# Metaformer kernel on one core: block 0 normalised by POOL, first maxima moved ahead of block 1's products, router chains reordered

## The reference, cut to what matters

```python
x = x + _L0_conv_ref(_ln_c(x), ...)   # attention in windows of 14 x 14 (padded), 12 heads of 16, relative positions
t = t + _L0_ffn_ref(_ln_t(t), ...)    # 8 experts, best 2 of each token, 192 -> 768 -> 192, gelu
x = x + _L1_conv_ref(_ln_c(x), ...)   # attention over 3 x 3 neighbours at dilations 1, 2, 3
t = t + _L1_ffn_ref(_ln_t(t), ...)    # 8 experts, best 2, weights normalised
def _ln_c(v, eps=1e-06): return (v - mean(v)) / sqrt(var(v) + eps)      # over the 192 channels
attn = softmax(q * scale @ k + rel_h + rel_w)                            # of the first attention
gates = softmax(x_flat @ Wg + bg); topk_g, topk_i = top_k(gates, 2)      # the router
```

## Time and profile before

| what | us |
|---|---|
| median of three runs | 894.55 |
| profiled execution | 897.03 |
| its span | 895.2 |
| TensorE busy in the span | 787.2 (88%) |
| VectorE, ACT, POOL busy | 422.8, 311.8, 364.8 |
| first scores (L792) | 73.90 |
| logits of router 0 read (L1215) | 272.49 |
| logits of router 1 read (L1215) | 669.05 |

### The profile page before, as it was taken

The page is one execution under the profiler, slowest core; times in us unless marked ns, Lnnn a source line. Parts: engine busy times, 40 slices in busy tenths (PEclk is TensorE's granted clock), DMA queues, the critical chain, the costliest instruction groups (busy, mean ns, idle before and its releaser), DMA issues.

```text
span 895.2 us, 19348 instructions
## 1 busy us (share of the span) xinstructions
PE 787.2 (88%) x6140; PEld 666.0 (74%) x6141; DVE 422.8 (47%) x1000; ACT 311.8 (35%) x862; POOL 364.8 (41%) x795
## 2 busy tenths in 40 slices
PE   6997999999986999999992589998786999999990
PEld 3775888888773799999991359783673899999980
DVE  7243545557637433333324516997338333333325
ACT  3332545455524233333331550012240333333330
POOL 5862354340130666666652130000032566666640
PEclk8685899999986999999997599999997999999995
DMA  7492564565382111111114089500971111111116
GB/s 222 108 240 67 130 142 123 145 158 103 133 327 95 45 46 46 45 51 50 51 38 141 1 217 232 80 24 27 322 266 72 38 51 48 48 51 46 45 28 211
DMA packets 60858, 96.50 MB, mean 108 GB/s; under 512 B 26223, under 2 KB 44356, under 8 KB 60808
## 3 DMA queue, kind: packets, MB, share of 16 engines
q1 hardware_dynamic: 42248, 59.60, 24.3%
q0 software_dynamic: 18560, 36.24, 13.9%
HBM read 65.51 MB, written 31.52 MB: 108 GB/s over the span
## 4 chain that ended last, share of the span: by engine, by line
PE 64%; DVE 15%; issue 6%; DMA 5%; POOL 4%; ACT 3%; SPq 2%; DVEq 0%; POOLq 0%
PE ps L1398 14%; PE ps L1406 10%; PE ps L1410 7%; PE ps L1774 4%; PE ps L747 3%; PE ps L723 3%; DVE x_sb L1340 2%; PE ps L772 2%; PE ps L1389 2%; PE ps L1792 2%; PE ps L792 2%; DVE arena L1686 2%; PE ps L380 2%; PE ps L816 2%; PE ps L858 1%
## 5 line engine op out<-in xcount | busy, mean ns | idle before, releaser
L1440 ACT ACTIVATE arena<-ps,b1s 128x128 f32<-128x128 f32 x468 | 129.5, 376 | 254.4 <-PE ps L1410 153.8
L1398 PE MATMUL ps<-arena 128*128 x936 | 165.4, 327 | 1.5 <-DVE rt L1305 1.5
L1398 PEld LDWEIGHTS ps<-arena 128*128 128x128 f32 x936 | 150.3, 190 | 2.4 <-issue 2.1
L1406 PE MATMUL ps<-xnT 128*128 128x128 f32 x936 | 117.5, 275 | 3.0 <-DVE xnT L1298 3.0
L1406 PEld LDWEIGHTS ps<-xnT 128*128 128x128 f32 x936 | 114.4, 192 | 4.0 <-DVE xnT L1298 4.0
L272 POOL TENSOR_TENSOR rstd<-veps,cst 128x4 f32<-128x4 f32 (+1 forms) x10 | 11.5, 1154 | 201.5 <-DVE veps L266 201.5
L603 DVE TENSOR_REDUCE rt<-ps 98x2 f32<-98x392 f32 x96 | 53.2, 563 | 79.7 <-PE ps L772 79.5
L1454 POOL TENSOR_TENSOR credit<-credit 1x1 f32<-1x1 f32 x306 | 57.8, 189 | 77.0 <-DVE rt L1305 34.3
L1462 POOL DMA_INDIRECT xnT<-xnd,gcur x78 | 78.6, 1007 | 16.2 <-issue 14.9
L1007 ACT ACTIVATE arena<-ps 98x392 f32<-98x392 f32 x96 | 47.0, 499 | 84.6 <-PE ps L792 84.0
L1410 PE MATMUL ps<-xnT,rt 64*128 64x128 f32 x936 | 73.2, 289 | 0.0
(11 more groups left out here) (215 smaller groups left out, 1310.2 us busy)
## 6 DMA issues: line engine op xcount, KB each, us to landing
arena<-in_w SPq DMA_DIRECT2D x16, 576.0 KB, 7.6
arena<-in_w1a SPq DMA_DIRECT2D x16, 384.0 KB, 6.0
arena<-yd SPq DMA_DIRECT2D x8, 768.0 KB, 7.1
kk<-kd SPq DMA_DIRECT2D x48, 96.0 KB
qq<-qd SPq DMA_DIRECT2D x16, 264.0 KB
qd<-arena POOLq DMA_DIRECT2D x16, 224.0 KB, 5.8
qq<-qd SPq DMA_DIRECT2D x16, 192.0 KB
arena<-in_w1b SPq DMA_DIRECT2D x16, 192.0 KB, 6.5
```

Of the source, the lines that this page charges most:

```text
L1398: last = mm(ps[:, DOWN, 0:C], hidT[r][:, f, :], w2s[:, e, f, :], start=f == 0, stop=f == FT - 1)
L1406: mm(hidden(r, f), wcura[r][:, f * P:(f + 1) * P], xgT[:, 0, :], start=f < 2, stop=False, skip_group_check=True)
L1440: last = nc.scalar.activation(hidT[r][:, f, :], hidden(r, f), ACT.Gelu, bias=b1s[l][:, bass.ds(e * FT + f, 1)])
```

## The change

1. Block 0's inverse root is taken by POOL's power, as everywhere else; ACT's root and VectorE's reciprocal go. SP loads `cst` second, the key constants later. VectorE scales the query/key weights after the tiles. POOL waits with its casts until the tiles are done; the power of blocks 1 to 3 comes after block 0's t2. ACT's first key rows come after the first relative rows. Two of nine first fillers go.
2. SP issues block 0's stores of t0, t2, r0, r1.
3. TensorE starts on the maxima right after block 1's t0; t2 and the pieces of r0 and r1 follow between units (`between`), and the fillers go. The bank list follows. ACT copies r1 of block 1 after the first exponentials.
4. In router 0, only the moments stay in step 7; the tiles come after all slots. TensorE's tail has another order, and the transposes alternate between banks 2, 3 and 0, 1.
5. In router 1, ACT copies block 3's values before it normalises block 0; transposes run a block ahead of the logits, in banks 6, 7 and 0, 1, with fillers of half the columns; twelve fillers, not nine, stand before the first transposes.

The diff, cut to its core:

```diff
         def ln_refine(v, n, bs):
...
-            if n == 0:
-                nc.vector.reciprocal(r, r).then_inc(s_("ln_inverse"), 1)
-                v.wait_ge(s_("ln_inverse"), turn)
...
+        def nx_bank(l, b):
+            return (2, 0)[b % 2] if l == 0 else (6, 0)[b % 2]
...
-            if b:
-                pe.wait_ge(s_("nx_copied"), 2 * (l * BLKS + b))
+            if b >= 2:
+                pe.wait_ge(s_("nx_copied"), 2 * (l * BLKS + b - 1))
+            if l == 1 and b == 1:
+                pe.wait_ge(s_("proj1_out"), 3)
...
+            for kind in ("t0", "t2", "r0", "r1"):
+                sp.wait_ge(s_("split"), split_at(kind, 0))
+                store(sp, kind, 0)
             sp.wait_ge(s_("q_rows"), CPB + 1)
             for cc in range(CPB):
                 load(0, cc)
...
             nc.gpsimd.memset(q0[32:64].bitcast(F32), 0.0).then_inc(s_("q_rows"), 1)
+            pool.wait_ge(s_("cst_in"), 16)
+            pool.wait_ge(s_("q_rows"), 1)
+            ln_power(pool, 0, first)
             pool.wait_ge(s_("cq_in"), 16)
-            pool.wait_ge(s_("q_rows"), 1)
+            pool.wait_ge(s_("xn_ready"), 1)
...
                 heads_split("t2", b)
+                if b == 0:
+                    ln_power(pool, 0, rest)
...
                 if b == BLKS - 1 and s == 7:
                     v.wait_ge(s_("misc_full"), max(FULL["x1", b], FULL["r2", b]))
-                    ln_moe(v, 0, range(BLKS - 1))
+                    ln_moments(v, 1, range(BLKS - 1))
...
+            moe_normalise(v, 0, range(BLKS - 1))
             normalise(BLKS - 1, 2)
...
-            keep_clock(BANK["r2", 0], 9)
+            keep_clock(BANK["r2", 0], 7)
...
             queries_and_keys(1, 0)
-            queries_and_keys(1, 2)
-            relatives(1, 0)
-            relatives(1, 1)
...
+            def between(H, u):
+                if (H, u) == (0, 2):
+                    queries_and_keys(1, 2)
+                if H == 2 and u < 2:
+                    relative(1, 0, u)
+                if (H, u) == (HC, 0):
+                    transposed_maxima(0)
+                if H == HC and u:
+                    relative(1, 0, u + 1)
+                if H == HC + 1 and u < 2:
+                    relative(1, 1, u)
+                if H == HC + 2 and u < 2:
+                    relative(1, 1, u + 2)
+
             for H in range(AHEAD):
                 for u in range(UNITS):
                     scores_for_max(H, u)
-                    mm(ps[:, PV, 0:2 * P], trib, maskb[:, 0, 0:2 * P], start=True, stop=True)
-                if H == HC:
-                    transposed_maxima(0)
+                    between(H, u)
...
-            nx_transpose(pe, 0, 0)
             transposed_outputs(BLKS - 1, 0)
             for part in range(2):
                 values_product(GROUPS - 1, part)
+            nx_transpose(pe, 0, 0)
+            token_major(BLKS - 1, 2)
             nx_transpose(pe, 0, 1)
-            token_major(BLKS - 1, 2)
+            transposed_outputs(BLKS - 1, 1)
             router_logits(pe, 0, 0, 0, 2)
-            transposed_outputs(BLKS - 1, 1)
-            router_logits(pe, 0, 0, 2, TPB)
             projection(BLKS - 1, 0)
             projection(BLKS - 1, 1)
+            router_logits(pe, 0, 0, 2, TPB)
             router_logits(pe, 0, 1)
             nx_transpose(pe, 0, 2)
+            mm(ps[:, PV, :], ident, cst[:, 0:BT], start=True, stop=True)
             router_logits(pe, 0, 2)
...
-            act.wait_ge(s_("ck_in"), 16)
-            for cc in range(2):
-                key_rows(cc)
-            ln_sqrt(act, 0, first)
...
             round_heads(0, 0)
-            ln_sqrt(act, 0, rest)
             round_heads(0, 2)
             copy_relative(0, 0)
+            act.wait_ge(s_("ck_in"), 16)
+            for cc in range(2):
+                key_rows(cc)
...
+                nx_transpose(pe, l, 0)
                 for b in range(BLKS):
-                    nx_transpose(pe, l, b)
-                    mm(ps[:, 5, :], ident, cst[:, 0:BT], start=True, stop=True)
+                    if b + 1 < BLKS:
+                        nx_transpose(pe, l, b + 1)
+                    mm(ps[:, 5, 0:BT // 2], ident, cst[:, 0:BT // 2], start=True, stop=True)
...
-            for _ in range(9):
+            for _ in range(12):
                 nc.tensor.matmul(ps[:, 4, :], ident, cst[:, 0:BT], start=True, stop=True)
...
-            for b in range(3):
+            for b in range(BLKS):
                 copy_values(b)
             block_normalise(act, 3, 0)
-            copy_values(3)
```

More of the change, by code:

```diff
@@ L491, in split_at, with store @@
             return b * len(SPLIT) + SPLIT.index(kind) + 1
+        def store(eng, kind, b):
+            for to, rows, heads, src, m, p0, p1 in stores(kind):
+                eng.dma_start(to[b, rows, heads].rearrange("r h n -> h r n"), src[p0:p1, m].bitcast(F32))\
+                    .then_inc(s_(f"{STORED[kind]}{b}"), 16)
         def first_matrices(sp, l, lo, hi):
@@ L541, in attn0_pool @@
         def attn0_pool(pool):
-            def store(kind, b):
-                for to, rows, heads, src, m, p0, p1 in stores(kind):
-                    pool.dma_start(to[b, rows, heads].rearrange("r h n -> h r n"), src[p0:p1, m].bitcast(F32))\
-                        .then_inc(s_(f"{STORED[kind]}{b}"), 16)
             def heads_split(kind, b):
@@ L1071, in attn0_scalar @@
             copy_relative(1, 0)
-            copy_relative(1, 1)
             def slot_a(b, s):
```

50 lines of the change are left out of this document (25 added, 25 removed).

## The result

Four runs of the changed kernel took 876.38, 879.18, 880.49 and 889.12 us (median 879.84), four of the kernel before 893.41 to 896.85 (median 895.28): ratio 0.9846, 95% interval [0.9809, 0.9883]. Six more runs of it later took 874.67 to 891.44 (0.9872 [0.9831, 0.9913]); all ten have a median of 882.9. So the change makes the kernel faster, by 12 to 15 us (under 2%, but clear of noise); forecast were 24.3. Medians here are over all runs of a kernel; the ratios leave out those over 1.5% above its fastest (three of the six of "late maxima", and one each of the changed kernel again, of "fillers before the maxima loop" and of "POOL stores").

The account below looks back on a forecast made before the run. TensorE was taken to bound the kernel (64% of the chain of waits, DMA 5%). Gains 11.9 + 4 + 3.7 + 4.7 = 24.3 took the profiled 897.03 to 872.7, less 2.5 to the median: 870.3 us, range 861 to 881.

Parts of the forecast that it names:

- the term of 4: First heads, 70 to 97 us: without the 5.30 us wait the stretch may run at full clock; 4 us, bounds 0 and 8.
- the step from the profiled execution to the median: End of the sum: the profiled execution before lay 2.5 us over its median, so 872.7 becomes 870.3.
- Part 1: Block 0's normalisation: transposes start at 9.6 us, not 16.20; window-order products at 17.2, not 25.74, 8.5 earlier.
- The rule on shared ports: Front: VectorE's two-input SBUF sum and POOL's SBUF reads exclude each other; POOL's splits may stand 3.2 us, otherwise nothing.
- Part 2: Stores by SP: POOL saves 3.6 us ahead of the last split; SP loads at 31 to 34 us, not 41.52.
- Part 3: Maxima first: first maxima at 40 to 43 us, first scores at 62; gain 11.9, bounds 8.5 and 16.
- the forecast's other chain: Front: block 0's last stores, SP's fourteen loads, then the maxima's row, ending at 58 to 65.4 us; 62 taken.
- first rival: Front: loads and maxima's row still end last, at 66, TensorE waits and drops clock; gain 16, 878.5 us, chance 0.18.
- Parts 4 and 5: End of first attention gains 3.7 us (bounds 1 and 6); second router gains 4.7 (bounds 3 and 6).
- the clock holds everywhere: Rival, whole kernel: scores start at 60 us, then gains of 8, 6 and 5.5; 861 us, chance 0.15.

Follow-up runs that it names:

- late maxima: Changed kernel with part 3 undone: all of block 1's products before the first maxima, the 18 loop fillers back; 884.32 us, ratio 0.9821.
- the changed kernel again: Changed kernel run six more times with no edit; 885.41 us, ratio 0.9872.
- fillers before the maxima loop: Changed kernel plus seven idle TensorE products of 512 columns ahead of the first maxima; 880.09 us, ratio 0.9862.
- POOL stores: Changed kernel with block 0's stores of t0, t2, r0 and r1 given back to POOL; 888.06 us, ratio 0.9922.
- first trace: Profiled execution of the changed kernel, unedited, the fastest of its first four; span 874.6 us.
- second trace: Profiled execution of the changed kernel run again without edit, the fastest of those six; 874.67 us.
- Filling that wait alone: Changed kernel with part 3 undone and only four idle products before the first scores; 883.75 us, ratio 0.9863.
- fillers in heads 0 to 2 alone: Four idle products in block 0's first three heads only: on the changed kernel 883.85 us, with part 3 also undone 877.52 us.
- sibling kernels: The experiments' variants of the changed kernel, with parts undone or fillers added; medians 868.48 to 888.54 us.
- early maxima with front fillers: Changed kernel plus seven idle products before the maxima loop and four in heads 0 to 2; 878.82 us, ratio 0.9825.
- late ones: Changed kernel with part 3 undone, four idle products before the first scores and four in heads 0 to 2; 868.93 us, ratio 0.9711.
- all fillers: Idle products before first maxima or scores, in first heads and both routers: changed kernel 871.08 us, with part 3 undone 868.48 us.

## Why the prediction was wrong

Forecast were 870.3 us (861 to 881); the first four runs give 879.84, just inside the range, all ten 882.9, outside it. The sign and most mechanisms held. What failed is the clock, in three places: in the loop of maxima (part 3), in the first heads (the term of 4), and in the step from the profiled execution to the median. The last is the largest.

**Part 1** held: transposes at 10.63 (forecast 9.6), L730 at 12.49 (12.6), L754 at 17.03 (17.2). That L730 came on time is luck in part: the fillers ended 1.2 us later than forecast and held the transposes, and VectorE's scaling beside POOL's casts, allowed 1.0, took 0.15 us an instruction and cost nothing. The 12-element power took 2.28 us (2.3).

**The rule on shared ports.** POOL's cast at 21.68 ran beside the padding key's sum and took 1.86 us, where the next of its kind took 0.61. That agrees with the Trainium skill, "SBUF — State Buffer", section "Who interferes with whom". It cost POOL 1.3 us, inside the 0 to 3.2 allowed, and SP still loaded at 32.80. One pair in the same rows does not fit: that sum started at 19.91 while POOL's power, which reads SBUF too, ran from 19.45 to 21.73, and it took the 3.16 us that it had taken with POOL idle.

**Part 2** held, and undoing it costs 5 us by the medians. SP's own issue was mis-sized: its eight stores of block 0 were issued from 18.72 to 28.12 and took 0.65 to 1.0 us each, not 0.40; little waited behind them.

**Part 3 failed in the first trace.** "After t0 maxima may start at 40 if the first chunk is in; SP's loads begin 31 to 34, so 40 to 43": the first chunk takes 9.4 to 12.4 us from first issue to first use, 12.4 there, which makes 45.20. The earlier trace rows did not hold that duration, and the sum took from the loads' start to the chunk as 9. Then the loop: the forecast gave 16 at full clock to 22 at half and took a middle, though the 6 us stand ahead of it sends the clock down at 41.8, and it took 22.5. First scores at 67.67, gain 6.2 for 11.9. In the second trace the same step came out: chunk at 43.13, scores at 62.51, gain 11.4. There the maxima's row decides, as the forecast's other chain had it (58 to 65.4, 62 taken). The runs show further that the reordering itself is worth nothing (late maxima: 63.87), since that chain ends at 62.5 to 66 in either order; the gain of the front is that of parts 1 and 2. That was the first rival, "SP's chain decides", at 0.18, and its time, 878.5, was the nearest. The wait for the row by which it was to be known shows in the second trace (3.28 us for 5.30); in the first the wait stood at the first chunk instead.

**The clock term of 4** gave 0.7 and 1.0 in the two traces; some 18.5 us at half clock stayed in that stretch. It is real in size, 4.6 to 7 with fillers, but the forecast hung it on one wait. Filling that wait alone brought nothing (171.3 us from first to last scores); fillers in heads 0 to 2 alone brought the stretch to 166.3 behind a loop at half clock and to 166.9 behind a stand of 3.8 us.

**Parts 4 and 5** were right in mechanism and gave 6.2 and 6.1 in the profiled execution for 3.7 and 4.7. In part 4 the projection ended 9.6 us after the last scores (248.53) where it took 14.5: 4.9, forecast 4.0. Block 3's chain to the transposes kept its 6.0 us, and from there to the read it took 4.9 in place of 6.2: the full clock in the transposes (1.06 us for 1.92), of which the forecast took 0.4 out of a possible 2.6. In traces of the sibling kernels these stretches run partly at half clock and give back up to 6 us in router 0 and 6 to 10 in router 1.

**The step from the profiled execution to the median is the largest miss.** The terms alone gave 20.7 (first trace) and 22.4 us (second) of the 24.3. That the first comes so near is luck in part: the front and the clock gave 9.0 less than forecast, the two routers 3.9 more, and the stretch between them 1.5 that nobody forecast. The forecast took the profiled execution of before as 2.5 over its median and carried that over; the profiled executions of the changed kernel lay 3.5 and 10.7 us under the medians of their batches, 6.5 and 8.2 under that of all ten. The kernel before spread by 0.4% to 1.0% in the batches run, the changed one by 1.9% (874.67 to 891.44), and its profiled execution was the fastest of four. With the clock held by fillers the new order is worth 18 to 23 us (891.1 against 871.1 and 868.5, and by the ratios), near the 24.3; against the 12 measured on all ten, a typical execution of the changed kernel loses an estimated 6 to 10 of them to the clock. The chance of "the clock holds everywhere" (861, 0.15) was a bet on chance timing; what it needed was fillers, and with them came medians of 868.5 to 871.1, the fastest execution at 865.05.

Still open: what decides from one execution to the next where the clock falls, and where it falls in the longer executions of the changed kernel, of which none has a trace; and why early maxima with front fillers (878.82) stay 10 us above late ones (868.93), while with all fillers they differ by 2.6.

## What to carry to other kernels

When a wait on the bounding engine's chain is removed, look for the next arrival in the same chain (here the first chunk's landing, 9 to 12 us after the first issue, and behind it the maxima's row, which TensorE still waited for when the loop was done early) before a gain is booked. Taking out fillers together with reordering work is two changes: cost the new gap and the half clock behind it, and fill every stand of that stretch, the short ones too. Before two traces are compared stretch by stretch, compare the granted clock of the stretch: 6 us between two routers were 1 to 3 us of order and the rest clock. Judge a change by the median of many executions when its spread grows; a single trace of this kernel flattered it by up to 8 us.

## What was not expected of the hardware

- Time follows the mean granted clock from one execution to the next: 874.67 us at 0.928 and 891.44 at 0.905 with the same program.
- A chunk of seven DRAM loads was first used 9.4 to 12.4 us after its first issue, in traces of kernels with the same loads.
- SP's stores from SBUF took 0.65 to 1.0 us of issue each, POOL's 0.6; SP's loads took 0.40 each in the first four of a chunk (1.61) and 1.0 in the next three (3.06).
- A VectorE sum of two SBUF inputs took 3.16 us both with POOL idle and begun during POOL's 12-element power, though it held POOL's cast up by 1.3 us.
- Fillers made the program shorter: four in the routers by 7 us, eight in the front of the version with late maxima by 15, though each costs TensorE 0.9 us (3.60 for four). On the kernel before, sixteen gave 4 us. They do not hold the clock every time: with all fillers one trace still had 10.2 us at half clock in router 0.
